# Attention core: the tensor engine's list cut into finer pieces, one head's scores by query at a time between them

## The reference

```python
x = x + 0.5 * ffn(layernorm(x))          # mixture of experts, 16 experts, top 4
x = x + attn(layernorm(x))
x = x + 0.5 * ffn(layernorm(x))

def attn(x, Wqkv, bqkv, Wo, bo):         # x: 4 x 512 x 256, 16 heads of 16
    q, k, v = heads(split(x @ Wqkv + bqkv))
    scores = einsum('bhid,bhjd->bhij', q, k) / sqrt(16)
    scores = scores - slope[h] * (i - j), and -inf where j > i
    attn = softmax(scores, axis=-1)
    out = einsum('bhij,bhjd->bhid', attn, v)
    return out @ Wo + bo
```

## Time and profile before

| what | us |
|---|---|
| median of 3 runs | 1133.45 |
| lowest and highest run | 1133.41, 1135.13 |
| the profiled execution's own time | 1132.82 |
| its span in the profile | 1131.1 |
| the attention core (first `take_max` to the end of the last `add_out`) | 506.7 to 726.3 |
| TensorE busy, share of the span | 739.4 (65%) |
| VectorE busy | 621.4 (55%) |
| ScalarE busy | 424.0 (37%) |

### The profile page before, as it was taken

The page is one execution under the profiler, slowest core; times in us unless marked ns, Lnnn a source line. Parts: engine busy times, 40 slices in busy tenths (PEclk is TensorE's granted clock), DMA queues, the critical chain, the costliest instruction groups (busy, mean ns, idle before and its releaser), DMA issues. The chain is left out here.

```text
span 1131.1 us, 22067 instructions
## 1 busy us (share of the span) xinstructions
PE 739.4 (65%) x5770; PEld 450.2 (40%) x5770; DVE 621.4 (55%) x1953; ACT 424.0 (37%) x945; POOL 368.1 (33%) x404
## 2 busy tenths in 40 slices
PE   2222068999999305757999999522204999999930
PEld 1121035666666202322353534421202666666620
DVE  5865046566665386336767673371601566665537
ACT  2322045555555202112646455111102555555510
POOL 3766712333333202450000000055672333333320
PEclk9999989999999756775999999755556999999975
DMA  8555322333333453430111110212232333333346
GB/s 303 202 181 180 122 60 74 86 94 96 82 91 97 140 180 96 144 102 2 45 31 45 31 31 3 76 69 89 80 116 75 92 96 95 92 95 94 82 144 228
DMA packets 110387, 114.31 MB, mean 101 GB/s; under 512 B 38836, under 2 KB 96669, under 8 KB 110272
## 3 DMA queue, kind: packets, MB, share of 16 engines
q1 hardware_dynamic: 95008, 73.82, 23.0%
q0 software_dynamic: 15264, 39.10, 9.3%
HBM read 60.89 MB, written 55.56 MB: 103 GB/s over the span
## 5 line engine op out<-in xcount | busy, mean ns | idle before, releaser
L319 POOL DMA_INDIRECT y_rows<-y_m,goal_m x158 | 155.7, 985 | 312.5 <-ACT y_m L482 292.3
L391 PE MATMUL banks<-w1s,rT_m 128*128 x948 | 236.0, 386 | 0.0
L666 DVE TENSOR_SCALAR b_m<-banks 128x256 f32<-128x256 f32 x158 | 67.0, 424 | 212.3 <-ACT p_m L468 126.9
L309 POOL DMA_INDIRECT x_rows<-row_m,row_to_m x128 | 132.5, 1035 | 124.5 <-DVE row_to_m L626 87.0
L1191 DVE CUSTOM_DVE_ANT_0 junk<-banks,maskq 128x128 bf16<-128x128 f32 (+3 forms) x256 | 115.7, 488 | 44.9 <-PE banks L1040 41.7
L461 ACT ACTIVATE rT_m<-banks 128x512 f16<-128x512 f16 x158 | 93.6, 592 | 111.5 <-issue 58.1
L391 PEld LDWEIGHTS banks<-w1s,rT_m 128*128 128x128 f16 x948 | 94.3, 99 | 98.5 <-issue 6.7
L413 PE MATMUL banks<-w2s,hT_m 128*128 x948 | 129.7, 273 | 0.0
L1160 ACT ACTIVATE probs<-banks 128x1024 f32<-128x1024 f32 (+3 forms) x128 | 86.0, 703 | 88.8 <-PE banks L1076 88.7
L373 PE MATMUL banks<-ident,rows_m 128*128 128x128 f16 x632 | 62.7, 223 | 78.0 <-DMA rows_m<-x_rows 40.5
L468 ACT ACTIVATE p_m<-banks 128x256 f32<-128x256 f32 x158 | 60.5, 383 | 110.5 <-PE banks L391 107.7
(11 more groups left out here) (164 smaller groups left out, 1157.9 us busy)
## 6 DMA issues: line engine op xcount, KB each, us to landing
rows_m<-x_rows SPq DMA_DIRECT2D x158, 128.0 KB
arena_m<-y_rows SPq DMA_DIRECT2D x32, 512.0 KB, 5.5
arena_m<-in_w SPq DMA_DIRECT2D x16, 512.0 KB, 6.5
arena_m<-in_w SPq DMA_DIRECT2D x16, 256.0 KB, 7.0
qk_split<-w_raw SPq DMA_DIRECT2D x32, 128.0 KB
x_rows<-pad SPq DMA_DIRECT2D x2, 2040.0 KB, 8.4
q_stack<-qk_split SPq DMA_DIRECT2D x32, 96.0 KB
k_stack<-qk_split SPq DMA_DIRECT2D x32, 96.0 KB
```

The source lines that it names most:

```text
L309: pool.indirect_dma_start(x_rows[m], bass.IndirectOffsetOnAxis(ap=row_to[:, i, k:k + 1], axis=0), row[:, i % NR, :], None).then_inc(scatte ...
L319: pool.indirect_dma_start(y_rows[m], bass.IndirectOffsetOnAxis(ap=goal[:, c, :], axis=0), y[:, n % NY, :], None, bounds_check=K * T - 1, o ...
L391: mm = pe.matmul(o, rT[:, n % 2, 2 * r + k, :], w1s[:, bass.ds(e, 1), k, w, :], start=False, stop=(k == HC - 1 and w == 1))
L666: dve.tensor_scalar(b[:, n % 2, :], bank[2 + n % 2][:, INNER:], (LIMIT + 1.0) * S, (1.0 - LIMIT) * S, ALU.min, ALU.max).then_inc(ev("b"), 1)
```

## The change

The lists of TensorE, ScalarE and VectorE in the core are written in another order. On TensorE the blocks between the scores become pieces, and they stand behind single `score_q` instead of behind pairs: parts 2 and 3 of the weighing apart (behind u = 0 and 2), `turn_max` behind u = 4, `spread_sums` behind u = 6, parts 0 and 1 each as two halves of two heads (behind u = 8 and 9, and 14 and 15), each pair of the projection as four quarters of 2 matmuls (behind u = 10 to 13), and the second pair a step later than the first. ScalarE's copy to `maxT` moves from behind the second `exp` to behind `copy_o` and the fourth `exp`. VectorE's `divide` comes one k later and `add_out` in the step behind its projection. `oT` gets a sixth buffer. No arithmetic is added or left out.

```diff
@@ -947,7 +947,7 @@
                                 mm.then_inc(s("v_product"), 1)
-                NU, U, KS, NO = B * QG, HG * TPB, 2 * TPB, 5
+                NU, U, KS, NO = B * QG, HG * TPB, 2 * TPB, 6
                 MAX_SCALE = 64.0
                 probs = [tmp(f"probs{j}", [P, HG, SEQ - j * P]) for j in range(TPB)]
                 mx = tmp("mx", [P, 2, TPB, HG])
@@ -1046,8 +1046,8 @@
                             pe.wait_ge(s("max"), n * U + U)
                             if n >= 4:
                                 pe.wait_ge(s("oT"), n - 3)
-                            if n >= 7:
-                                pe.wait_ge(s("x"), (n - 3) // QG * 2)
+                            if n >= QG + 3 and n % QG in (3, 0):
+                                pe.wait_ge(s("x"), (n - QG - 3) // QG * 2 + 1 + (n % QG == 0))
                             for i in range(TPB):
                                 mm = pe.transpose(bank[7][0:HG, i * P:(i + 1) * P], mx[:, n % 2, i, :], ident[:, :])
                             mm.then_inc(s("max_turned"), 1)
@@ -1078,18 +1078,19 @@
                                                skip_group_check=True)
                             mm.then_inc(s("scores_k"), 1)
-                        def weigh(n, j):
-
-                            if j == 0:
+                        def weigh(n, j, heads):
+
+                            if j == 0 and heads[0] == 0:
                                 pe.wait_ge(s("v_near"), n + 1)
                                 if n:
                                     pe.wait_ge(s("o_copied"), n)
                             pe.wait_ge(s("exp"), n * KS + 2 * j + 2)
-                            for c in range(HG):
+                            for c in heads:
                                 mm = pe.matmul(bank[6][32 * c:32 * c + DV, j * P:], v_near[:, n % 2, j, c, :],
                                                probs[j][:, c, :], start=(j == 0), stop=(j == TPB - 1),
                                                tile_position=(0, 32 * c), skip_group_check=True)
-                            mm.then_inc(s("weighed"), 1)
+                            if heads[-1] == HG - 1:
+                                mm.then_inc(s("weighed"), 1)
                         def spread_sums(n, turned):
@@ -1097,22 +1098,45 @@
                             pe.wait_ge(s("maxT"), turned)
                             if n:
                                 pe.wait_ge(s("oT"), n)
+                            if n == NU - 3:
+                                pe.wait_ge(s("x"), 2 * (B - 1))
                             pe.matmul(bank[7][:, :], spread_sum[:, :], oT[:, n % NO, :], start=True, stop=True)\
                               .then_inc(s("sums_spread"), 1)
-                        def project_out(b, pair):
-                            pe.wait_ge(s("wo_loaded"), 16)
-                            pe.wait_ge(s("oT"), b * QG + QG)
-                            if pair:
-
-                                pe.wait_ge(s("x"), b * 2 + 1)
-                            for t in (2 * pair, 2 * pair + 1):
-                                for g in range(QG):
-                                    mm = pe.matmul(bank[7][:, t % 2 * H:(t % 2 + 1) * H],
-                                                   oT[:, (b * QG + g) % NO, t * P:(t + 1) * P],
-                                                   wos[:, g, :], start=(g == 0), stop=(g == QG - 1),
-                                                   skip_group_check=True)
-                            mm.then_inc(s("out_product"), 1)
+                        def project_out(b, pair, quarter):
+                            if quarter == 0:
+                                pe.wait_ge(s("wo_loaded"), 16)
+                                pe.wait_ge(s("oT"), min(b * QG + QG + pair, NU))
+                                if pair:
+
+                                    pe.wait_ge(s("x"), b * 2 + 1)
+                            t = 2 * pair + quarter // 2
+                            for g in (quarter % 2 * 2, quarter % 2 * 2 + 1):
+                                mm = pe.matmul(bank[7][:, t % 2 * H:(t % 2 + 1) * H],
+                                               oT[:, (b * QG + g) % NO, t * P:(t + 1) * P],
+                                               wos[:, g, :], start=(g == 0), stop=(g == QG - 1),
+                                               skip_group_check=True)
+                            if quarter == 3:
+                                mm.then_inc(s("out_product"), 1)
+
+                        def between(n, u):
+
+                            if 1 <= n <= NU:
+                                if u == 0:
+                                    weigh(n - 1, 2, range(HG))
+                                if u == 2:
+                                    weigh(n - 1, 3, range(HG))
+                            if u == 4 and n + 1 < NU:
+                                turn_max(n + 1)
+                            if u == 6 and 2 <= n < NU + 2:
+                                spread_sums(n - 2, min(n + 2, NU))
+                            if n < NU:
+                                if u in (8, 9):
+                                    weigh(n, 0, range(u % 2 * 2, u % 2 * 2 + 2))
+                                if u in (14, 15):
+                                    weigh(n, 1, range(u % 2 * 2, u % 2 * 2 + 2))
+                            if n > QG and n % QG in (1, 2) and u in (10, 11, 12, 13):
+                                project_out(n // QG - 1, n % QG - 1, u - 10)
                         pe.wait_ge(s("tables"), 16)
                         for u in range(U):
@@ -1120,26 +1144,14 @@
                         turn_max(0)
                         for u in range(U):
                             score_q(1, u)
-                        for n in range(NU + 2):
+                        for n in range(NU + 3):
                             for k in range(KS):
                                 if n < NU:
                                     score_k(n, k)
-                                if n + 2 < NU:
-                                    score_q(n + 2, 2 * k)
-                                    score_q(n + 2, 2 * k + 1)
-                                if k == 1 and n + 1 < NU:
-                                    turn_max(n + 1)
-                                if k == 1 and 1 <= n <= NU:
-                                    weigh(n - 1, 2)
-                                    weigh(n - 1, 3)
-                                if k == 3 and 2 <= n:
-                                    spread_sums(n - 2, min(n + 2, NU))
-                                if k == 5 and n < NU:
-                                    weigh(n, 0)
-                                if k == 7 and n < NU:
-                                    weigh(n, 1)
-                                if k in (4, 6) and n >= QG + 1 and n % QG == 1:
-                                    project_out(n // QG - 1, (k - 4) // 2)
+                                for u in (2 * k, 2 * k + 1):
+                                    if n + 2 < NU:
+                                        score_q(n + 2, u)
+                                    between(n, u)
                     @block.scalar
                     def _(act):
@@ -1172,10 +1184,10 @@
                             for k in range(KS):
                                 if n < NU:
                                     exp(n, k)
-                                if k == 1 and n + 1 < NU:
-                                    rows_of_max(n + 1)
                                 if k == 2 and n >= 1:
                                     copy_o(n - 1)
+                                if k == 3 and n + 1 < NU:
+                                    rows_of_max(n + 1)
                     @block.vector
                     def _(dve):
@@ -1212,18 +1224,18 @@
                         for n in range(2):
                             for u in range(U):
                                 take_max(n, u)
-                        for n in range(NU + 2):
+                        for n in range(NU + 3):
                             for k in range(KS):
                                 if n + 2 < NU:
                                     take_max(n + 2, 2 * k)
                                     take_max(n + 2, 2 * k + 1)
-                                if k == 3 and n >= 2:
+                                if k == 0 and n > QG + 1 and n % QG in (2, 3):
+                                    add_out((n - 2) // QG - 1, n % QG - 2)
+                                if k == 4 and 2 <= n < NU + 2:
                                     divide(n - 2)
                                 if k == 6 and 1 <= n <= NU:
                                     invert(n - 1)
-                                if k in (4, 6) and n >= QG + 1 and n % QG == 1:
-                                    add_out(n // QG - 1, (k - 4) // 2)
-
+                        add_out(B - 1, 1)
         moe(0)
         end_phase()
```

## The result

The changed kernel takes 1176.06 us, the median of 4 runs (1172.76 to 1180.65), against 1134.29 for the kernel before in 4 runs on the same chip (1133.41 to 1137.54). The ratio is 1.0366, with an interval of 1.0324 to 1.0407: 41.8 us slower. The forecast was 1171, with 1150 to 1183 around it.

The account below looks back on a forecast made before the run. TensorE's list sets the pace, sharing the bound with VectorE through 1.84 us of bank waits per plain step. Dearer halves, the wait at `maxT` and quarters summed over the steps to +37.7 on 1132.8: 1171 us, range 1150 to 1183.

Parts of the forecast that it names:

- The plain step: Core step without projection: TensorE work 10.9, wait at `maxT` 1.3, bank waits 1.0; 13.1 us against 10.39, +2.7.
- The stall: TensorE's `spread_sums` stands from 3.9 to 5.2 us in a step, waiting for ScalarE's copy to `maxT`: +1.3.
- B: Weighing halves: two heads cost half of four, or ways in and out are hidden; about 1150 us, chance 0.12.
- C: No wait at `maxT`, ScalarE's copy comes in time; 13 x 1.3 less, about 1154 us, chance 0.12.
- E: No change: B and C in part, bank gains against what is lost; about 1133 us, chance 0.03.
- D: Faster: scores between short pieces feed VectorE and end bank waits; needs B and C both; 1112 us, chance 0.07.
- Bank waits: TensorE's scores 12 and 13 wait for banks `take_max` holds: 1.0 us of 1.84 remains in a plain step.
- The sum: All steps of the core together: +37.7 us on 1132.8, giving 1171 us.
- Steps 2 to 4: Three plain steps of the core, each 2.7 us longer: +8.1.
- Steps 5 to 12: Two sequences, each with a projection pair of steps (+5.5) and two plain steps (+5.4): +21.8 us.
- Step 14: No new scores by query, so halves cost nothing; it gains a projection pair and the wait at `maxT`: about +5 us.
- Steps 0 and 1: Start of the core: no sums to spread, so no wait at `maxT`; halves paid, partly at lower clock: +3.5 us.

Follow-up runs that it names:

- the last four runs: Changed kernel again, 1123.26 us; whole pieces behind every second score with the copy early, repeated, 1072.21; that kernel with matmuls added ahead of the core, 1076.34, or in tail, 1070.49.
- both parts undone: Against the changed kernel: parts 0 and 1 of the weighing whole again and ScalarE's copy to `maxT` early again; 1090.35 us, ratio 1.011 to the kernel before.

## Why the prediction held, step by step

**The plain step: right.** Forecast 13.1, measured 13.11 (steps 3, 4, 8 and 12). Its terms hold one by one: the halves cost two whole weighings (0.97 and 0.97, 0.76 and 0.75); with the halves alone in the kernel before, 0.98 and 0.97. The measured 0.97 against 0.99 also bears out the rule cited from the Trainium skill, page "TensorE: Matmul & The Clock Gate", section "Part 3: Packing small matmuls — row/col tiling", by which tiles that run together take one matmul's time and a few ns for each more: two more heads are 0.02 here. In the tail, where no score stands between the halves, they run as one again:

```profile
748.88 1.05 PE L1089 MATMUL banks<-probs,v_near 128*17 128x512 f32 x8
```

**The stall: right.** Forecast from 3.9 to 5.2, 1.3; measured 1.35, with the copy over at 5.17 and named by the trace in step 2. Taking it away gave back 1.34 a step, and it alone in the kernel before cost 1.4. Rivals B and C, which each take one of these terms away, are thereby out, and with them E and D, which are built on them.

**Bank waits: right.** I left 1.0 to scores 12 and 13, and by the distances between starts they wait 0.46 and 0.56. The idle times that the profile marks there, 0.30 and 0.39, are the smaller count.

**The sum: right in sign and mechanism, 4 low.** Against 37.7, 41.8 was measured. The largest miss is the clock, for which the sum had no term. By terms, from the table of steps:

- Steps 2 to 4: +8.2, forecast 8.1.
- Steps 5 to 12: 122.1 against 97.3, +24.8, forecast 21.8. The quarters were a little mis-sized: a projection step took 16.75 where I had 16.6 (a pair then costs 16.75 - 13.11 + 1.0 of covered waits = 4.6 for my 4.4), and the second one of a sequence 17.01. The quarters alone in the kernel before cost 1.6 a step. The same 0.26 is in the plain step behind them, 13.37. In both steps `add_out` stands near the start of VectorE's list, and the score ahead of `turn_max` waits 0.22 for VectorE; the prediction had let `add_out` lie under TensorE's pieces at no cost. And **the clock did not stay at 1.00**, as I had written: 18.60 - 17.01 = 1.6 in step 6.
- Step 14: +7.0, forecast +5. The wait before `spread_sums` is 1.91 there, and the clock behind it falls: in the 5 us behind it the granted clock is 0.66, and the weighing of 512 columns takes 1.80 for 1.05 and the first half of the pair 2.65 for the second's 1.99, some 1.4 together:

```profile
735.29 1.10 PE L1103 MATMUL banks<-oT,spread_sum 128*128 128x512 f32 x2 [1.91 <-issue]
...
736.62 1.80 PE L1089 MATMUL banks<-probs,v_near 128*17 128x512 f32 x8
```

```profile
731.00:736.00 5.00, 3.09 (x40) 1.32 (x32) 0.01 (x1) 4.19 (x6) 0.41 (x1) 1.00 0.00 0
736.00:741.00 5.00, 5.00 (x28) 2.48 (x28) 0.94 (x2) 1.19 (x2) 0.00 (x0) 0.66 0.03 4
```

- Steps 0 and 1: +2.0, forecast +3.5. A part of that is luck: step 0 ran at a clock of 0.71 where it had 0.56 before. Step 13: -0.5, forecast -0.7.

These make 41.5, and the last 0.3 to 0.4 lie in step 15 and the tail. The range held the result, but its upper end was worked out from dearer quarters, stalls and ways in; the clock, worth some 3 us in steps 6 and 14, was not in it. That it stayed inside is in part luck. On the chip of the last four runs the change cost 45.9, against an upper end of 50.

**What the experiments added that the prediction did not have.** The terms are not additive. The halves alone cost 2.1%, the late copy alone 2.85%, the quarters 0.5%, but the whole change 4.2%; and undoing the halves alone gained nothing. TensorE's clock ties them. With the same late copy it falls in one to three of the twelve steps from 2 to 13 with the halves in place, in eight of them in the kernel before, and in all twelve with the weighing whole again. Whether the halves keep it up by their own work or by covering bank waits (the 0.60 is there without them) these runs don't separate. Why it fell in step 6 and not in step 10, which has the same list, stays open too, and so does why it fell in other steps on the other chip.

## What to carry to other kernels

Matmuls that run side by side in strips of the array share one pass, here four heads in 0.99 us and two in 0.97: cutting such a group in two and putting other work between costs the whole price twice, so move whole groups, and cut only what runs one after the other. Before a small copy is moved later on an idle engine, follow it to the in-order list that waits for it: moving 0.57 us of ScalarE made TensorE stand for 1.35 us in each step. And when work is removed around a wait, look at the granted clock before believing the timing: here the kernel with less work was no faster until the wait was filled.

## What the runs showed of the hardware

- **Waits well under 2 us can cost the clock.** Behind waits of 1.35 and 0.60 us TensorE went from 2.4 to 1.2 GHz for some 3 us, in each of twelve steps of one kernel (longer in those with a projection), and five added matmuls of 0.25 each took most of that away: three falls were left. In the kernel with both parts undone it fell twice behind waits of 0.60, 0.30, 0.39 and 0.22 alone.
- **Keeping TensorE busy did not bring it back in the head.** With added matmuls it was busy 8.59 and 8.85 of 10 us there, and the clock stayed at 0.50.
- **Two float32 matmuls side by side cost what four do**: 0.97 against 0.99 for 512 columns, 0.76 against 0.77 for 384.
